# Gated unit and the second mixture's norm, routing and scatters by chunks; the root mean square from two logarithms

## What is computed

```python
x = x + 0.5 * ffn(ln(x))        # two layers of local attention and gated MLP
x = x + ssm(ln(x))              # state space layer
x = x + 0.5 * ffn(ln(x))
x = x + 0.5 * moe(ln(x))        # mixture: 8 experts, 2 per token
x = x + unit(ln(x))             # gated unit
x = x + 0.5 * moe(ln(x))
```

```python
def unit(x):
    rms = norm(x, axis=-1) * 128 ** -0.5
    xn = x / (rms + 1e-8)
    u = silu(xn @ u_w.T + u_b)
    v = silu(xn @ v_w.T + v_b)
    return (u * (v * t_zero)) @ o_w.T + o_b + x
def moe(x):
    probs = softmax(x @ w_router)
    weights, idx = top_k(probs, 2)
    # each token goes through its two experts:
    # gelu(x @ w1[e] + b1[e]) @ w2[e] + b2[e], summed by weights
```

## Time and profile before

| | us |
|---|---|
| median of 3 runs | 1226.49 |
| lowest, highest | 1225.02, 1232.32 |
| the profiled execution | 1228.67 |
| its span, first to last instruction | 1226.9 |

### The profile page before, as it was taken

One profiled execution on the slowest core, in us unless ns is written; L12 is line 12 of the kernel. 1 busy time (PEld: TensorE's weight loads), 2 busy tenths in 40 slices (PEclk: granted clock), 3 DMA queues, 4 the chain that ended last, 5 costly groups with the idle time before them and its releaser, 6 DMA issues.

```text
span 1226.9 us, 25914 instructions
## 1 busy us (share of the span) xinstructions
PE 1024.7 (84%) x9078; PEld 632.6 (52%) x9078; DVE 733.6 (60%) x1629; ACT 682.6 (56%) x1292; POOL 525.9 (43%) x405
## 2 busy tenths in 40 slices
PE   3789999999998776899999999999369967705995
PEld 1345555555554363455555555554269942404885
DVE  0567676777775642776767767686644417561442
ACT  2566676667664553667567557655246634503552
POOL 2655555455341442544443444422635500073441
PEclk9899999999999968999999999999679987957998
DMA  9895444364343501544433444433112230011223
GB/s 344 262 302 129 94 98 94 88 139 101 88 92 65 67 2 33 125 105 106 105 92 84 111 98 98 94 88 155 43 50 67 61 87 0 20 50 48 62 67 116
DMA packets 88943, 120.57 MB, mean 98 GB/s; under 512 B 20368, under 2 KB 72336, under 8 KB 87920
## 3 DMA queue, kind: packets, MB, share of 16 engines
q1 hardware_dynamic: 82256, 96.84, 32.9%
q0 software_dynamic: 6272, 20.44, 4.5%
q10 hardware_dynamic: 288, 1.63, 0.3%
HBM read 63.21 MB, written 22.11 MB: 70 GB/s over the span
## 4 chain that ended last, share of the span: by engine, by line
PE 60%; ACT 15%; issue 9%; DVE 8%; DMA 3%; POOL 3%; SPq 1%; DVEq 0%; ACTq 0%; POOLq 0%
PE banks L980 6%; PE banks L970 6%; PE banks L601 6%; PE banks L672 5%; PE banks L686 5%; PE banks L761 3%; PE banks L647 3%; PE banks L630 3%; POOL moe_rows L1903 3%; PE banks L679 3%; ACT arena L1155 3%; PE banks L731 2%; PE banks L736 2%; PE banks L1001 2%; ACT arena L1165 2%
## 5 line engine op out<-in xcount | busy, mean ns | idle before, releaser
L1931 POOL TENSOR_TENSOR arena<-arena 128x1024 f32<-128x1024 f32 x64 | 150.8, 2357 | 336.8 <-DVE arena L1568 333.2
L1920 POOL TENSOR_TENSOR arena<-arena 128x1024 f32<-128x1024 f32 x64 | 150.9, 2358 | 42.1 <-ACT arena L1155 42.1
L1147 ACT ACTIVATE arena<-banks,arena 128x512 f32<-128x512 f32 x128 | 80.7, 681 | 94.9 <-PE banks L679 94.6
L601 PE MATMUL banks<-arena 128*128 128x512 f32 x256 | 126.7, 619 | 6.7 <-DVE arena L1486 5.9
L1560 DVE TENSOR_REDUCE arena<-banks 128x4 f32<-128x512 f32 x128 | 82.6, 687 | 80.6 <-PE banks L630 80.0
L1910 POOL DMA_INDIRECT moe_outs<-arena x78 | 81.6, 1046 | 101.8 <-DVE arena L1819 88.3
L1903 POOL DMA_INDIRECT moe_rows<-arena x64 | 65.3, 1020 | 138.1 <-DVE arena L1541 120.1
L1363 ACT ACTIVATE arena<-banks,arena 128x128 f32<-128x128 f32 x312 | 89.3, 371 | 59.8 <-PE banks L970 59.5
L1568 DVE TENSOR_TENSOR arena<-arena 128x1024 f32<-128x1024 f32 x64 | 78.1, 1220 | 27.4 <-DMA arena<-arena 27.4
L980 PE MATMUL banks<-arena 128*128 x624 | 87.1, 283 | 4.6 <-ACT arena L1363 4.5
L1160 ACT ACTIVATE arena<-banks 128x1024 f32<-128x1024 f32 x64 | 65.7, 1027 | 44.1 <-PE banks L601 43.2
(11 more groups left out here) (216 smaller groups left out, 1972.0 us busy)
## 6 DMA issues: line engine op xcount, KB each, us to landing
arena<-arena SPq DMA_DIRECT2D x256, 128.0 KB, 3.8
arena<-rstd SPq DMA_DIRECT2D x128, 256.0 KB, 4.2
moe_rows<-arena POOLq DMA_DIRECT2D x12, 903.0 KB, 6.3
arena<-moe_rows SPq DMA_DIRECT2D x78, 64.5 KB
arena<-in_rot SPq DMA_DIRECT2D x4, 1024.0 KB, 11.4
arena<-in_mw SPq DMA_DIRECT2D x2, 2048.0 KB, 10.8
arena<-moe_outs SPq DMA_DIRECT2D x16, 256.0 KB, 4.9
arena<-ssm_a SPq DMA_DIRECT2D x4, 512.0 KB, 6.1
```

What stands on the lines that cost most here:

```text
L601: mm(bank[k], w_qkv[d][:, w0:w0 + P], src, start=True, stop=True).then_inc(proj, 1)
L1920: nc.gpsimd.tensor_tensor(TA[:, n % 2], RAW, ROTV[:, :, 0, c * C:(c + 1) * C], ALU.mult).then_inc(cos_done, 1)
L1931: nc.gpsimd.tensor_tensor(TA[:, n % 2], TA[:, n % 2], TB, ALU.add).then_inc(rot_sum, 1)
```

## The change

- The unit's Sqrt, addition of 1e-8 and reciprocal go. The mean of squares v is already in the norm's bank. ACT takes Ln(v + 1e-5) and Ln(v + tiny), DVE subtracts them, and ACT takes Exp(0.5 * difference), which is the root mean square of the normed chunk, then Ln of that plus 1e-8, then Exp of minus that. The second squaring and mean matmul go too.
- The first mixture's combining (`combine`), the unit and the second mixture's norm, routing and ranking are interleaved by chunk in one list on each of PE, ACT and DVE. The scatters' list is the same.
- The projections rotate over three banks instead of four; the second mixture centres all its chunks in bank 7.
- The unit's weights load right after the last row load of the first mixture; the second loading of the router's weights and biases goes. The combined rows `YC` and the gates `UV` get places of their own.
- PRE gets one row more, which takes one step from the tile map.

The core of the diff (the removed lines of the unit and of the mixture's lists stand in the functions printed above; of the three new `unit` functions, for PE, ACT and DVE in this order, the added lines are shown):

```diff
-        MX_CEN, MX_VAR = [(0, 3, 7, 3), (0, 1, 2, 3)], [(1, 4, 6, 5), (4, 5, 6, 7)]
+        MX_CEN, MX_VAR = [(0, 3, 7, 3), (7, 7, 7, 7)], [(1, 4, 6, 5), (3, 4, 5, 3)]
+        SN0 = 2 * NCH
...
+                    if run == 0:
+                        sp.dma_start(WU, ins["unit"]).then_inc(unit_in, 16)
                     for b in range(4):
                         sp.wait_ge(outs_out[b], uses(b, run, NT) * 16)
...
-                if kind == "U":
-                    x_whole(sp, k)
-                    sp.dma_start(WU, ins["unit"]).then_inc(unit_in, 16)
...
+            def unit(mix):
+                def mixed(c):
                     if c >= 2:
+                        pe.wait_ge(sn_out, SN0 + c - 1)
+                    combine(0, c, 4 + c % 2)
+                def unit_centred(c):
+                    pe.wait_ge(x_moe, c + 1)
+                    mm(bank[4 + c % 2][:], centre, X[:, c * C:(c + 1) * C], start=True, stop=True).then_inc(sn_cen, 1)
+                def unit_variance(c):
+                    pe.wait_ge(sn_sq, SN0 + c + 1)
                     if c:
+                        pe.wait_ge(sn_log, SN0 + 2 * c)
+                    mm(bank[6][:], mean, HC, start=True, stop=True).then_inc(sn_var, 1)
+                def up(c, parts=range(4)):
+                    if c == 0:
+                        pe.wait_ge(unit_in, 16)
+                    pe.wait_ge(xn_done, c + 1)
+                    for k in parts:
+                        q = 4 * c + k
+                        if q >= 3:
+                            pe.wait_ge(uv_silu, q - 2)
+                        if c >= 2 and k == 0:
+                            pe.wait_ge(unit_sum, 2)
+                        mm(bank[q % 3][:], WU[:, k * P:(k + 1) * P], H2[:, c * C:(c + 1) * C], start=True, stop=True).then_inc(uv_mm, 1)
+                def down(c):
+                    pe.wait_ge(gated, 2 * c + 2)
+                    if c == 2:
+                        pe.wait_ge(sn_log, SN0 + 2 * NCH)
+                    for k in range(2):
+                        last = mm(bank[UO_BANK[c]][:], WU[:, 4 * P + k * P:4 * P + (k + 1) * P], UV[:, c % 2, k],
+                                  start=(k == 0), stop=(k == 1))
+                    last.then_inc(uo_mm, 1)
+                def mix_centred(c):
+                    pe.wait_ge(x_unit, c + 1)
+                    if c:
+                        pe.wait_ge(xtok_done, 2 * NCH + 2 * c)
+                    centred(X, c, MX_CEN[1][c])
+                def mix_variance(c):
+                    if c == 0:
+                        pe.wait_ge(unit_sum, 1)
+                    elif c < 3:
+                        pe.wait_ge(sn_out, SN0 + c + 2)
+                    else:
+                        pe.wait_ge(rank_dve, RANK_STEPS * (NCH + 1))
+                    variance(mix, c, MX_VAR[1][c])
+                mixed(0)
+                unit_centred(0)
+                mixed(1)
+                unit_variance(0)
+                unit_centred(1)
+                unit_variance(1)
+                mixed(2)
+                up(0)
+                unit_centred(2)
+                mixed(3)
+                up(1)
+                unit_variance(2)
+                down(0)
+                unit_centred(3)
+                mix_centred(0)
+                mix_variance(0)
+                down(1)
+                unit_variance(3)
+                route(mix, 1, 0)
+                mix_centred(1)
+                mix_variance(1)
+                rank(1, 0)
+                route(mix, 1, 1)
+                up(2, range(3))
+                rank(1, 1)
+                up(2, range(3, 4))
+                up(3)
+                down(2)
+                down(3)
+                mix_centred(2)
+                mix_variance(2)
+                route(mix, 1, 2)
+                mix_centred(3)
+                mix_variance(3)
+                rank(1, 2)
+                route(mix, 1, 3)
+                rank(1, 3)
 
...
+            def unit(mix):
+                def unit_square(c):
+                    act.wait_ge(sn_cen, SN0 + c + 1)
+                    if c:
+                        act.wait_ge(sn_var, SN0 + c)
+                    A(HC, bank[4 + c % 2][:], ACT.Square).then_inc(sn_sq, 1)
+                def unit_logs(c):
+                    act.wait_ge(sn_var, SN0 + c + 1)
+                    if c:
+                        act.wait_ge(sn_mid, NCH + c)
+                        act.wait_ge(sn_out, SN0 + c)
                     if c >= 2:
+                        act.wait_ge(xn_done, c - 1)
+                    A(ta, bank[6][:], ACT.Ln, bias=eps_c).then_inc(sn_log, 1)
+                    A(UT[c % 2], bank[6][:], ACT.Ln, bias=tiny_c).then_inc(sn_log, 1)
+                    act.wait_ge(sn_log, SN0 + 2 * c + 1)
+                    A(UR, ta, ACT.Exp, scale=-0.5, bias=zero_c).then_inc(sn_rstd, 1)
+                def unit_scale(c):
+                    v = UT[c % 2]
+                    act.wait_ge(sn_mid, NCH + c + 1)
+                    A(v, v, ACT.Exp, scale=0.5, bias=zero_c).then_inc(rms_act, 1)
+                    act.wait_ge(rms_act, 3 * c + 1)
+                    A(v, v, ACT.Ln, bias=floor_c).then_inc(rms_act, 1)
+                    act.wait_ge(rms_act, 3 * c + 2)
+                    A(v, v, ACT.Exp, scale=-1.0, bias=zero_c).then_inc(rms_act, 1)
+                def silu(c):
+                    act.wait_ge(unit_in, 16)
                     if c >= 2:
                         act.wait_ge(uo_mm, c - 1)
                     for k in range(4):
+                        q = 4 * c + k
+                        act.wait_ge(uv_mm, q + 1)
+                        A(UV[:, c % 2, k], bank[q % 3][:], ACT.Silu, bias=WU[:, 6 * P + k:6 * P + k + 1]).then_inc(uv_silu, 1)
+                def mix_square(c):
+                    norm_square(mix, c, MX_CEN[1][c])
+                def mix_root(c):
+                    norm_root(mix, c, MX_VAR[1][c])
+                unit_square(0)
+                unit_logs(0)
+                unit_square(1)
+                unit_scale(0)
+                unit_logs(1)
+                unit_scale(1)
+                silu(0)
+                unit_square(2)
+                silu(1)
+                log_exp_table()
+                unit_logs(2)
+                mix_square(0)
+                unit_square(3)
+                mix_root(0)
+                unit_scale(2)
+                tokens(1, 0)
+                unit_logs(3)
+                mix_square(1)
+                unit_scale(3)
+                mix_root(1)
+                tokens(1, 1)
+                silu(2)
+                silu(3)
+                log_exp_table()
+                mix_square(2)
+                mix_root(2)
+                tokens(1, 2)
+                mix_square(3)
+                mix_root(3)
+                tokens(1, 3)
 
...
+            def unit(mix):
+                def log_ratio(c):
+                    v = UT[c % 2]
+                    dve.wait_ge(sn_log, SN0 + 2 * c + 2)
+                    TT(v, v, ta, ALU.subtract).then_inc(sn_mid, 1)
+                def unit_normed(c):
+                    dve.wait_ge(sn_rstd, SN0 + c + 1)
+                    TT(YB[:, c * C:(c + 1) * C], bank[4 + c % 2][:], UR, ALU.mult).then_inc(sn_out, 1)
+                def scaled(c):
+                    cc = slice(c * C, (c + 1) * C)
+                    dve.wait_ge(rms_act, 3 * c + 3)
+                    dve.wait_ge(sn_out, SN0 + c + 1)
+                    TT(H2[:, cc], YB[:, cc], UT[c % 2], ALU.mult).then_inc(xn_done, 1)
+                def gates(c):
+                    dve.wait_ge(uv_silu, 4 * c + 4)
+                    for k in range(2):
+                        STT(out=UV[:, c % 2, k], in0=UV[:, c % 2, k], scalar=WU[:, 6 * P + 4 + k:6 * P + 5 + k],
+                            in1=UV[:, c % 2, 2 + k], op0=ALU.mult, op1=ALU.mult).then_inc(gated, 1)
+                def added(c):
+                    cc = slice(c * C, (c + 1) * C)
+                    dve.wait_ge(uo_mm, c + 1)
+                    after(dve, x_unit, c)
+                    STT(out=US, in0=bank[UO_BANK[c]][:], scalar=WU[:, 6 * P + 6:6 * P + 7], in1=YB[:, cc],
+                        op0=ALU.add, op1=ALU.add).then_inc(unit_sum, 1)
+                    dve.wait_ge(unit_sum, c + 1)
+                    TT(X[:, cc], X[:, cc], US, ALU.add).then_inc(x_unit, 1)
+                def mix_normed(c):
+                    norm_chunks(mix, plain, [c])
+                update(0, 0, 4)
+                update(0, 1, 5)
+                log_ratio(0)
+                unit_normed(0)
+                scaled(0)
+                log_ratio(1)
+                unit_normed(1)
+                update(0, 2, 4)
+                scaled(1)
+                gates(0)
+                update(0, 3, 5)
+                added(0)
+                gates(1)
+                log_ratio(2)
+                unit_normed(2)
+                mix_normed(0)
+                added(1)
+                scaled(2)
+                route(1, 0)
```

(21 more changed lines are left out.)

215 lines of the change are left out of this document (49 added, 166 removed).

## The result

| | before | after |
|---|---|---|
| median of the runs, us | 1227.33 (1225.02 to 1232.32, 4 runs) | 1211.12 (1208.15 to 1217.26, 4 runs) |
| profiled execution, us | 1228.67 | 1217.26 |
| its span, us | 1226.9 | 1215.5 |

The ratio is 0.987, with a 95% interval of 0.982 to 0.992. The changed kernel was run ten more times beside the experiments; over all 14 executions its median is 1211.8, between 1199.67 and 1219.12. The profiled one of the first four is the slowest of those four.

What follows compares the result with a forecast made beforehand. The rewritten 122.5 us was bound by reciprocals (13.4 us on DVE) and 32 scatters (41.32 us) with nothing left to hide behind. 24.0 saved less 11 for the clock gave 13.0 less: 1213.5 us, own range 1207 to 1219.

Steps and rivals of the forecast that it cites:

- The wait before the fourth projection: Chunk 0 in the unit: PE waits about 3.0 us for the first Silu, since projections rotate over three banks.
- Legs at full clock: Four parts laid out from first combining to second mixture's last scatter; that scatter starts at 1088.1 against 1112.10, 24.0 us less.
- leg 1: From the combining to chunk 2's first Silu: ACT works 35.7 us, stands 10.9 more, reaching Silu at 1042.0.
- The clock: PE's half clock after pauses, at four places in the rewritten part: costs 11 us, between 0 and 31.
- Rival one: In the rewritten part the clock holds because combines and projections fill PE's pauses: 1202.5 us, chance 0.14.
- the likeliest case: Whole kernel: 24.0 us saved less 11 for the lower clock, giving 1213.5 us, chance 0.52.
- the stretch: First mixture's first combining matmul to second mixture's last scatter: 122.5 us before, forecast 24.0 less at full clock.
- The larger part is order: Combining through scatters run by chunks, so scatters of chunks 0 and 1 start while 2 and 3 are in the unit.
- the sixteen hidden scatters: Second mixture's scatters of chunks 0 and 1, begun at 1036.2 and issued by 1056.6, under the unit.
- Leg 4: From chunk 2's slots to the last scatter: 15 steps of 1.272 us plus slowdowns, 20.5 us.
- the cover of the diagonal's work: After chunk 3's slots: tile map, expert weights and L1834, 14.8 us, stay hidden with 2.5 us to spare.
- The tile loop: Second mixture's loop over 39 tiles, after the rewritten part: to stay at 94 us, else the forecast is wrong.

Runs made afterwards that it cites:

- the second measurement: The changed kernel run again unaltered, on a different chip from the third measurement: median 1203.07 us, ratio 0.981 to the kernel before.
- the third: Profile of the changed kernel run unaltered a third time, beside versions made from it: median 1217.64 us, ratio 0.988 to the kernel before.
- the math alone: Kernel before with Sqrt, addition and reciprocal replaced by Ln/Exp, second squaring and mean matmuls dropped, old chunk order kept: 1216.52 us, ratio 0.990.
- the order alone: Changed kernel with the 1e-8 addition and reciprocal back on DVE in place of one Ln and one Exp on ACT: 1224.58 us, ratio 0.995.
- the new order for the end: Changed kernel with gates 3 ahead of chunk 2's sum, and chunk 3's centring and variance ahead of chunk 2's route and rank: 1205.03 us, ratio 0.980.
- a held-back version: Changed kernel with GpSimd's second-mixture scatters held until all four chunks have their slots: 1240.05 us, ratio 1.010 to the kernel before.

## Why the prediction was right, and what in it was not

**The time.** Forecast 1213.5, measured 1211.1. With the second measurement of the same kernel, 1203.1, it would have missed its own range of 1207 to 1219, so part of the hit is luck. Of the signs named ahead, the first scatter was to come at 1038 to 1041, which is 48.4 to 51.4 after the combining's start: 50.8, 46.6 and 50.9. GpSimd's pause of over 10 us: 18.1, 13.8 and 18.5. The last scatter after 107.4 to 110.4, or 98.5 if the clock holds: 108.8, 100.5 and 109.6. The wait before the fourth projection, forecast as 3.0: 2.5. The half clock, forecast for 36 to 50 us after the combining's start and from 68 on, stood in the first profile from 22.1 to 25.4, from 42.6 to 56.1 and, but for some 3 us, from 66.6 on.

**Legs at full clock: right as far as can be seen.** They were to make 98.5 us, and the second profile, whose clock was highest, took 100.5, with 2.1 too much in the leg whose clock was 0.70. No profile had full clock throughout. ACT's 51 instructions of leg 1 were laid out as 35.7 us and add up to 35.7; from its first Square to the first Silu of chunk 2 it took 50.6, 47.4 and 50.7 where 46.6 were laid out. Table loads cost 1.30 each again, as the timeline of ACT in the first profile after shows:

```profile
1014.54 1.28 ACT L1427 ACT_TABLE_LOAD   x1
1015.84 2.59 ACT L1427 ACTIVATE arena<-banks,arena 128x512 f32<-128x512 f32 x4
```

The dearer switch that the Trainium skill names (ScalarE: Activation LUTs, What ACT_TABLE_LOAD costs) was not paid here either.

**The clock: right in size for two profiles of three, wrong in kind.** I took 11 as the likely value of one number. It differs from execution to execution of one kernel: 10.3, 2.0 and 8.5, the last without the 2.6 us of DVE's unexplained wait. Rival one (the clock holds: 1202.5) and the likeliest case (1213.5) were thus the same kernel at different times; the second measurement's median of 1203.1 looks like the one and the first's of 1211.1 like the other, though more than half of the difference between their profiles lies ahead of the stretch. The forecast argued from pauses of 3.00 and 4.75 us. Here the clock fell behind the 2.5 us before the fourth projection in two of three profiles and held in the third. The rule on pauses that the forecast quotes from the Trainium skill stands on that page under Why this matters for your kernels.

**"The larger part is order": not borne out.** By ratios the math alone is worth 1.0% (0.5 to 1.5), the order alone 0.5% (0.2 to 0.8), both 1.2 to 1.9%. In the stretch, by one profile of each: math 11.1 us less, order 6.5, both together 13.7, 22.0 and 12.9. So on top of the math the order adds 2.6, 11.0 and 1.8, never more than the math by itself. By whole executions it stays open: beside the math alone, the unaltered kernel on the same chip was 13.4 us faster, by its two other medians 5.4 faster and 1.1 slower. The step that failed is that I priced the removed reciprocals only inside the new order and never laid out the old one without them. There, DVE's list lets the first gates start ten us earlier.

**What the order gives and takes.** Count chunk 3's slots and the last scatter from the combining's start. Before: 93.2 and 122.5. Math alone: 82.1 and 111.5. Changed: 98.4, 90.3 and 99.1 for the slots (86.3 forecast), 10.2 to 10.5 more for the last scatter. So the order saves 18.9 us between the last slots and the last scatter (29.3 becomes 10.2 to 10.5, the sixteen hidden scatters of the forecast), and pays 8 to 17 of them back, since the last slots come later than in the old order with the same math. How much is paid back goes with the clock.

**The last steps.** Leg 4 was forecast at 20.5 and took 20.1 to 20.4. From the last scatter to the first expert it is 5.73 to 5.98 us in place of 5.32, so the cover of the diagonal's work held to within 0.7, as in the forecast.

**The tile loop.** I had said I would be wrong if it changed. From the first expert to the combining it took 95.0 before and 90.6, 91.5 and 93.4 after; it was 94.4 with the math alone and 94.3 with the order alone, and 92.6 in the new order for the end. In the eight profiles of kernels made from the changed one by other edits, except for the one with the reciprocals, it lies between 91.4 and 94.3. The first mixture's loop, the same in all, lies between 88.6 and 91.7 in the profiles of the kernel before and of the changed one. Of the 11.4 us between the spans of the first two profiles, before and after, 13.7 came from the stretch and 4.4 from here; 6.1 were lost ahead of the stretch and 0.6 in the ways between. Nothing was run that tells whether the loop gains through the change or varies by itself; that stays open.

## What to carry to other kernels

Before an overlap is priced, lay out the old order with the slow operation taken away: what the engine's own list keeps behind it (here the gates, 6.9 us) can be worth as much as the new overlap. Two edits that meet on the same path want a run each, and a held-back version shows what the overlap alone is worth. Where pauses of TensorE can put its clock at half, give the clock's price as a spread between executions, judge by a median over many, and set a variant beside the unaltered kernel measured with it.

## What was not expected of the hardware

The same program's stretch of 100.5 us became 108.8 in one profile and 109.6 in another. In the first of these the granted clock (0.70 against 0.79) is what differs; in the second 2.6 us are a wait of DVE whose end the profile puts to no engine of the core. The mean clock of whole executions of the changed kernel (0.923 to 0.939) goes with their times, while for the kernel before it does not. Two Ln and two Exp of about 0.7 us each on ACT, in place of a Square and a Sqrt there and a reciprocal of 3.35 us on DVE, paid 12 us in the old order; in the new one, an Ln and an Exp in place of the reciprocal paid 7 to 13. And whether the clock falls is not told by where the pauses are alone: the pause of 2.5 us before the fourth projection was followed by a clock of 0.50 in two of the changed kernel's three profiles, and by 1.00 in the third.
